# Left sweeps of a convolution chain: the additions of residual and state go from GpSimd to VectorE, in pieces of 256 columns

## The reference

```python
def step(prev, row):
    new = row + jax.nn.relu(_conv1d(prev, w, b))
    return (new, new)
_, rest = jax.lax.scan(step, rows[0], rows[1:])
```

## Time and profile before

| | us |
|---|---|
| time, median of 3 runs | 3128.18 (3127.83 to 3134.39) |
| span of the profiled execution | 3124.2 |
| TensorE (PE) busy | 2751.9 (88%) |
| VectorE (DVE) busy | 2169.9 (69%) |
| ScalarE (ACT) busy | 1362.1 (44%) |
| GpSimd (POOL) busy | 301.7 (10%) |

### The profile page before, as it was taken

One profiled execution on the slowest core, in us unless ns is written; L12 is line 12 of the kernel. 1 busy time (PEld: TensorE's weight loads), 2 busy tenths in 40 slices (PEclk: granted clock), 3 DMA queues, 4 the chain that ended last, 5 costly groups with the idle time before them and its releaser, 6 DMA issues. The chain is left out here.

```text
span 3124.2 us, 71772 instructions
## 1 busy us (share of the span) xinstructions
PE 2751.9 (88%) x25712; PEld 2482.1 (79%) x25712; DVE 2169.9 (69%) x5176; ACT 1362.1 (44%) x2113; POOL 301.7 (10%) x816
## 2 busy tenths in 40 slices
PE   5888879999999999927988889878999999999791
PEld 4666669999999999923457667657999999999791
DVE  7888846666666667767028888786666666666865
ACT  3766642246632222236445566543225662222120
POOL 1112110000000001135000101010000000000602
PEclk9999989999999999968989999998999999999696
DMA  4333220000000000079247897956000000000758
GB/s 90 81 92 97 67 111 0 0 0 0 0 0 0 0 0 0 0 211 234 47 41 92 102 110 97 111 69 116 0 0 0 0 0 0 0 0 0 123 92 128
DMA packets 735623, 164.91 MB, mean 53 GB/s; under 512 B 728208, under 2 KB 728848, under 8 KB 730640
## 3 DMA queue, kind: packets, MB, share of 16 engines
q1 hardware_dynamic: 608640, 132.08, 24.4%
q10 hardware_dynamic: 126864, 31.19, 6.0%
HBM read 96.13 MB, written 67.11 MB: 52 GB/s over the span
## 5 line engine op out<-in xcount | busy, mean ns | idle before, releaser
L272 PE MATMUL L_conv<-L_x_hi,L_w_hi 128*128 128x256 f32 x5040 | 1249.4, 284 | 50.9 <-DVE L_w_lo L236 29.2
L272 PE MATMUL L_conv<-L_x_hi,L_w_lo 128*128 128x256 f32 x5040 | 1246.1, 282 | 0.0
L156 ACT ACTIVATE L_row_b<-S,L_bias 128x256 f32 (+1 forms) x1008 | 514.0, 510 | 1172.9 <-DVE L_x_hi L210 1162.0
L272 PEld LDWEIGHTS L_conv<-L_x_hi,L_w_hi 128*128 128x128 f32 x5040 | 958.0, 190 | 55.2 <-issue 29.3
L272 PEld LDWEIGHTS L_conv<-L_x_hi,L_w_lo 128*128 128x128 f32 x5040 | 956.9, 190 | 0.0
L220 DVE SCALAR_TENSOR_TENSOR S<-L_conv,L_neg_bias,L_row_b 128x256 f32 x1008 | 487.6, 484 | 498.7 <-PE L_conv L276 498.1
L276 PE MATMUL L_conv<-L_x_lo,L_w_hi 128*128 128x256 f32 x5040 | 769.6, 283 | 6.2 <-DVE L_x_lo L212 6.2
L276 PEld LDWEIGHTS L_conv<-L_x_lo,L_w_hi 128*128 128x128 f32 x5040 | 676.2, 190 | 9.8 <-DVE L_x_lo L212 9.7
L212 DVE TENSOR_TENSOR L_x_lo<-S,L_x_hi 128x256 fp32r<-128x256 f32 x1016 | 465.0, 458 | 34.7
L210 DVE TENSOR_SCALAR L_x_hi<-S 128x256 fp32r (+1 forms) x1016 | 322.7, 318 | 35.3
L607 PE MATMUL dc_conv<-dc_xz_hi,dc_w_hi 128*128 128x512 f32 x384 | 171.0, 445 | 6.5 <-DVE dc_w_lo L734 6.5
(11 more groups left out here) (204 smaller groups left out, 2909.4 us busy)
## 6 DMA issues: line engine op xcount, KB each, us to landing
dc_raw<-x SPq DMA_DIRECT2D x32, 512.0 KB, 6.5
x_scratch<-dc_raw SPq DMA_DIRECT2D x16, 1024.0 KB, 7.5
at_res<-x_scratch SPq DMA_DIRECT2D x32, 512.0 KB, 11.7
x_scratch<-at_res SPq DMA_DIRECT2D x64, 256.0 KB, 5.8
fs_buf<-x_scratch SPq DMA_DIRECT2D x32, 512.0 KB, 6.5
sh_G<-x_scratch ACTq DMA_DIRECT2D x56, 256.0 KB, 5.8
out<-fs_buf SPq DMA_DIRECT2D x32, 256.0 KB, 4.4
out<-fs_buf ACTq DMA_DIRECT2D x32, 256.0 KB, 4.8
```

The lines of the kernel that those rows point to most:

```text
L156: nc.scalar.activation(row_b[p][:, :, :], line(k, at_step(k, i), p), ACT.Identity, bias=bias[:, k:k + 1]).then_inc(row_b_ready[p], 1)
L272: nc.tensor.matmul(out, w[:, k, s * P:(s + 1) * P], x_hi[p][:, s:s + J, :], start=(s == 0 and n == 0), stop=False)
```

## The change

GpSimd makes no additions in the left sweeps any more; VectorE makes them, between half steps of the sweep. In layer 1 each 512-column addition becomes two of 256 (16 rows each), behind the two halves of one step, and the bn_stats follows between the halves of the step after it; a quarter so takes ten steps instead of five, and begins one step after the quarter is final. In layer 3 the loop runs over the first 31 steps, and the last 32 are written out: behind each of their 64 half steps stands a piece of 256 columns (8 rows of 32 columns), four of which are one item. SyncE's order is the same, but waits for four pieces an item. The final additions of items 16 to 31 stay as they are.

```diff
--- before.py
+++ after.py
@@ -201,8 +201,6 @@
             for k in range(1, 4):
                 pool.wait_ge(w_hi_ready, k)
                 nc.gpsimd.tensor_tensor(w_lo[:, k, :], w_raw[:, k, :], w_hi[:, k, :].bitcast(F32), ALU.subtract).then_inc(rest_ready, 1)
-            if final:
-                final.early_pool(pool, new_ready, done_before)
 
         @block.vector
         def _(dve):
@@ -873,10 +871,10 @@
     def load_residual(self, sp, n):
         sp.dma_start(self.xr[n % RING], self.x1[n].rearrange("p (i w) -> p i w", w=W)).then_inc(self.x1_in[n % RING], 16)
 
-    def add_quarter(self, eng, n, g):
+    def add_quarter(self, eng, n, g, rows=slice(0, J)):
         part = slice(g * QUARTER, (g + 1) * QUARTER)
-        cells = self.xr[n][:, :, part]
-        return eng.tensor_tensor(cells, cells, columns_of(self.S, n)[:, :, part], ALU.add)
+        cells = self.xr[n][:, rows, part]
+        return eng.tensor_tensor(cells, cells, columns_of(self.S, n)[:, rows, part], ALU.add)
 
     def quarter_stats(self, n, g):
         return self.nc.vector.bn_stats(self.bn[:, n, g, :], self.xr[n][:, :, g * QUARTER:(g + 1) * QUARTER])
@@ -884,15 +882,6 @@
     def early_sync(self, sp):
         for n in range(RING):
             self.load_residual(sp, n)
-
-    def early_pool(self, pool, new_ready, done_before):
-        for n in range(RING):
-            pool.wait_ge(self.x1_in[n], 16)
-        for g in (3, 2, 1):
-            for p in range(2):
-                pool.wait_ge(new_ready[p], done_before(3, STEPS - g * QUARTER))
-            for n in range(RING):
-                self.add_quarter(self.nc.gpsimd, n, g).then_inc(self.quarter_summed, 1)
 
     def early_vector(self, dve, step):
         def several(first, last):
@@ -902,14 +891,19 @@
 
         at = 0
         for g in (3, 2, 1):
-            ready = STEPS - g * QUARTER + RING + 1
+            ready = STEPS - g * QUARTER + 1
             several(at, ready)
             for n in range(RING):
-                step(3, ready + n, 0)
-                dve.wait_ge(self.quarter_summed, (3 - g) * RING + n + 1)
+                if g == 3:
+                    dve.wait_ge(self.x1_in[n], 16)
+                for half in range(2):
+                    step(3, ready + 2 * n, half)
+                    self.add_quarter(self.nc.vector, n, g, slice(half * J // 2, (half + 1) * J // 2)).then_inc(self.quarter_summed, 1)
+                step(3, ready + 2 * n + 1, 0)
+                dve.wait_ge(self.quarter_summed, 2 * ((3 - g) * RING + n + 1))
                 self.quarter_stats(n, g).then_inc(self.early_stats, 1)
-                step(3, ready + n, 1)
-            at = ready + RING
+                step(3, ready + 2 * n + 1, 1)
+            at = ready + 2 * RING
         several(at, STEPS)
 
     def pads(self):
@@ -1739,6 +1733,7 @@
 
 BUFS = 13
 PART = W // 2
+PIECES = 4
 ITEMS = 2 * B
 
 
@@ -1768,15 +1763,15 @@
             eng.dma_start(rows[q][:, :, self.columns(item)],
                           self.buf[item % BUFS][q * HALF:(q + 1) * HALF, :, :]).then_inc(self.stored[item % BUFS], 16)
 
-    def add(self, eng, item):
-        buf = self.buf[item % BUFS]
-        return eng.tensor_tensor(buf[:, :, :], buf[:, :, :], columns_of(self.S, item % B)[:, :, self.columns(item)], ALU.add)
+    def add(self, eng, item, rows=slice(0, J)):
+        cells = self.buf[item % BUFS][:, rows, :]
+        return eng.tensor_tensor(cells, cells, columns_of(self.S, item % B)[:, rows, self.columns(item)], ALU.add)
 
     def early_sync(self, sp):
         for item in range(BUFS):
             self.load(sp, item)
         for item in range(B):
-            sp.wait_ge(self.early_summed, item + 1)
+            sp.wait_ge(self.early_summed, PIECES * (item + 1))
             self.store(sp, item)
             if item >= 2:
                 self.load(sp, item - 2 + BUFS)
@@ -1784,16 +1779,14 @@
             self.load(sp, item)
 
     def early_vector(self, dve, step):
-        with dve.Fori(0, STEPS) as i:
+        with dve.Fori(0, STEPS - PART) as i:
             for p in range(2):
                 step(3, dve.snap(i), p)
-
-    def early_pool(self, pool, new_ready, done_before):
-        for p in range(2):
-            pool.wait_ge(new_ready[p], done_before(3, STEPS - PART))
         for item in range(B):
-            pool.wait_ge(self.loaded[item % BUFS], 16 * (item // BUFS + 1))
-            self.add(self.nc.gpsimd, item).then_inc(self.early_summed, 1)
+            dve.wait_ge(self.loaded[item % BUFS], 16 * (item // BUFS + 1))
+            for piece in range(PIECES):
+                step(3, STEPS - PART + (item * PIECES + piece) // 2, piece % 2)
+                self.add(self.nc.vector, item, slice(piece * J // PIECES, (piece + 1) * J // PIECES)).then_inc(self.early_summed, 1)
 
 
 POOL_ITEMS = [item for item in range(B, ITEMS) if item % 3 == 2]
```

## The result

The changed kernel takes 3094.5 us (median of four runs, 3088.7 to 3106.4) against 3131.3 before (3127.8 to 3142.3): ratio 0.9886, 95% interval 0.9855 to 0.9916. The prediction was 3092.6 us. The profiled execution has a span of 3087.7 us, against 3124.2 before and 3088.6 in the sum.

The account below looks back on a forecast made before the run. TensorE was taken to bound the sweeps at 1.77 us a half step, except where GpSimd's additions stall VectorE. Terms -35.3 - 9.3 + 0 + 0.5 + 8.5 = -35.6 us gave span 3088.6, plus 4.0: 3092.6 us, range 3085 to 3107.

Parts of the forecast that it names:

- The stall: Left sweeps: GpSimd's additions stretch VectorE's instructions and TensorE waits; 35.3 us lost in the second layer, 9.3 in the first.
- The pieces: Left sweeps: VectorE's 256-column additions, 0.58 us each and occupying 0.49, cost nothing, hidden by the wait for TensorE.
- The two-row line: Piece length estimated from VectorE additions of 1024 and 512 columns: 1.68 ns a column plus 0.15 us, giving 0.58 us.
- a wait for TensorE: Sign of being right: VectorE still waits a few hundredths of a us for TensorE, with updates 1.77 us apart.
- the cover: Second layer's left sweep: VectorE's half step of 1.68 us lies under TensorE's 1.77, 0.09 us to spare.
- Rival A: Left sweep: part of the pieces shows, VectorE setting the pace of 64 half steps; 3106 to 3120 us, chance 0.06.
- The end: End of the left sweep: last piece adds 0.5 us, SyncE's remaining stores and loads delay the final additions by 8.5.
- the high end: Upper bound for SyncE's delay at the sweep's end: 11.7 us, from stores and loads with a backlog in the queue.
- The tail: From the first final addition on: a stream of stores, no shorter or longer than before, 63 us.
- B: Left sweep: TensorE idles a little each half step and its clock falls, 2.99 us each; +78, 3171 us, chance 0.04.
- C: Left sweeps: the stall was not GpSimd's, so stretching stays or moves; 3128 us, plus or minus 6, chance 0.02.
- D: The end is cheaper or the stall was dearer: below 3084 us, chance 0.02.

Follow-up runs that it names:

- the memsets: The kernel before, with layer 3's 16 early GpSimd additions replaced by memsets of the same buffers; one run, 3092.3 us.
- The doubled pieces: The changed kernel, with a second addition of 256 columns into a spare buffer ahead of each layer 3 piece; profiled span 3116.9 us against 3087.7.
- The 512 kernel: The changed kernel, with layer 3 pieces of 512 columns behind every second half step; profiled span 3087.4 us against 3087.7.
- the second measurement: The changed kernel measured again on another occasion against the kernel before: 3096.7 against 3123.4 us, ratio 0.9919.

## Why the prediction was right

**The stall.** 35.3 us were forecast for the second layer, 35.4 came; 9.3 for the first, 9.6 came. The step that carried it, counting the half steps inside the stretched stretch and pricing them at TensorE's 1.77, needed no model of the contention, only the demonstration that GpSimd caused it; the memsets show that. Two things in the trace of the kernel before say what the 35 us consist of. Three of VectorE's updates in it:

```profile
2914.00 0.47 DVE L220 SCALAR_TENSOR_TENSOR S<-L_conv,L_neg_bias,L_row_b 128x256 f32 x1
...
2919.89 0.47 DVE L220 SCALAR_TENSOR_TENSOR S<-L_conv,L_neg_bias,L_row_b 128x256 f32 x1
...
2958.83 0.49 DVE L220 SCALAR_TENSOR_TENSOR S<-L_conv,L_neg_bias,L_row_b 128x256 f32 x1 [0.17 <-issue]
```

A half step takes 5.89 us while GpSimd adds, which is two of its additions of 47.20/16 = 2.95 us: one passes while x_lo is held, one while x_hi is. (GpSimd's first three end at 2913.79, 2916.81 and 2919.69; x_lo, x_hi and the next x_lo end 0.29, 0.15 and 0.28 us behind them.) The nine half steps up to 2958.83 lose 32.7 us in all. The last two, 2958.83 to 2965.03, come after GpSimd's last addition and still lose 2.7: TensorE is busy throughout, at its lower clock level (0.50 from 2958.83 to 2962.04).

**The pieces.** They cost nothing, as forecast: 64 half steps in 113.17 us, 1.768 each, against 1.77 without pieces. The size was a little low: 0.61 us against 0.58, occupying 0.53 against 0.49, which left 0.07 us and not 0.09. The two-row line itself was right: the last piece, which nothing follows, took its 0.58 (3013.14). Its rows were of additions outside the sweep, and amid the sweep additions of every size are longer: 0.61 against 0.58, 1.05 against 1.01, 1.97 against 1.87. What lengthens them is not shown. The forecast that VectorE still shows a wait for TensorE failed: behind the pieces the view shows none, the rest of the cover being a few hundredths. Rival A would have needed a piece occupying 0.60. The doubled pieces show what it would have been: of the second addition's 0.53 us, 0.07 are still covered, and the rest is paid 64 times.

**The cover is wider than I reasoned.** The prediction compared VectorE's half step with TensorE's as if each had to fit. The 512 kernel shows that only the mean must, while one half step may be 0.4 us late: an update comes due when TensorE has 1.77 us of the other half ahead, and the update and x_hi need 0.82 of them. How far this reaches was tried at one more point only: of 1.3 us of lateness with pieces of 1024, about 0.5 did not show.

**The end.** 0.5 for the last piece came as 0.5. For SyncE 8.5 us were forecast and 9.7 came, just above the 6 to 9.5 that I had added up and below the 11.7 of the high end. (The range of the forecast took 5 as this term's low end, where the sum gave 6; nothing hung on it.) The mis-sized part is the issue of the loads: two stores took 1.59 us, less than the 2.5 forecast, but the first two loads 4.92 and all three 7.64 in a row, where I had 2.5 to 4 for the first two. The tail from the first final addition was 62.9 us before and 63.0 after, as forecast.

**The rivals.** B, the falling clock, did not come: even with VectorE setting the pace and TensorE busy 36.70 of 40 us the granted clock stayed at 1.00. The Trainium skill, in "TensorE: Matmul & The Clock Gate", section "A second HAM failure mode", tells of a kernel in which short idle times between groups of matmuls make the clock go back and forth; here they did not. C fell with the change itself and with the memsets. D did not come either.

**What was luck.** That forecast and median lie 1.9 us apart says less than it seems. In the trace SyncE cost 1.2 us more than forecast, while the two stalls gave back 0.4 more and the stretches that the change doesn't touch were 1.9 shorter (-0.6 and -1.3 in the table): the errors cancel. And the second measurement's 3096.7 us lies 4.1 above the forecast, at a gain of 26.7 us and not 35.6. The terms of the sum are borne out by the positions in the traces, not by the time.

## What to carry to other kernels

An engine that is idle for 90% of the span can still be the most expensive place for work, if its instructions hold another engine that is on the path; look for instructions whose duration changes from row to row with the same shape. When work moves under a matmul-bound loop, sum what the engine has to do in a few turns against the matmuls of those turns, and let one instruction be late by no more than the matmuls that stand ahead, less what must still be made for the next ones (here 0.4 us of lateness was free, and 1.3 was not). And look at what the moved work now finishes last: a queue that has to issue transfers before a block may end holds all engines.

## What the runs showed of the hardware

VectorE's two-input subtraction is held by GpSimd's additions (0.43 to 3.00 us) and not by its memsets (0.43), while the x_hi product is held by both (0.29 to 2.45 and to 1.04). While GpSimd adds without a pause, each of the two ends just behind the end of one of its additions (2.95 us each), while the update, which reads the matmuls' output and one tensor in the on-chip memory, keeps its 0.47 us. An addition that reads one input with a stride of 16 elements takes 0.61 us for 256 columns, 1.05 for 512 and 1.97 for 1024 amid the sweep, and 0.58, 1.01 and 1.87 with nothing of the sweep behind it; two of 256 in a row start 0.53 us apart, 0.07 before the first one's end. With TensorE held up in every half step, 271 matmuls in place of 341 in 40 us, the granted clock stayed at 1.00.
